# The last expert stage of a two-layer gated block: where the second product is scaled, and which engine does it

## The reference, cut to what matters

```
gate_scores = xf @ gate_W + gate_b
topk_scores, topk_idx = top_k(gate_scores, 2);  weights = softmax(topk_scores)
expert:  h = relu(layernorm(xf @ w1 + b1) * g1 + be1)
         layernorm(h @ w2 + b2) * g2 + be2
out = sum(weights * exp_out) + xf
x = x + tanh(g_ffn[1]) * out
```

## Time and profile before

| | us |
|---|---|
| median of 3 runs | 2147.1 |
| lowest and highest | 2144.46, 2152.93 |
| the profiled execution | 2151.43 |
| its span in the profile | 2149.6 |
| PE busy in the span | 2058.6 (96%) |
| DVE busy | 1737.7 (81%) |
| ACT busy | 1394.5 (65%) |
| POOL busy | 1269.6 (59%) |

### The profile page before, as it was taken

The page is one execution under the profiler, slowest core; times in us unless marked ns, Lnnn a source line. Parts: engine busy times, 40 slices in busy tenths (PEclk is TensorE's granted clock), DMA queues, the critical chain, the costliest instruction groups (busy, mean ns, idle before and its releaser), DMA issues.

```text
span 2149.6 us, 57692 instructions
## 1 busy us (share of the span) xinstructions
PE 2058.6 (96%) x19788; PEld 1795.7 (84%) x19788; DVE 1737.7 (81%) x4788; ACT 1394.5 (65%) x2978; POOL 1269.6 (59%) x2056
## 2 busy tenths in 40 slices
PE   6999999999699999999699999999899999999997
PEld 5888888888599999999588888888788888888885
DVE  5889888888588888888577787777588888888886
ACT  4766666666487877878366666666566666666663
POOL 5787888887300000000477878777378878878786
PEclk9999999999799999999899999999999999999998
DMA  7555221221466666666322222222100000000000
GB/s 230 187 180 166 67 65 61 69 64 53 158 239 226 247 223 246 221 244 213 133 69 71 71 75 71 75 71 66 45 23 30 29 28 29 30 30 30 30 26 18
DMA packets 151664, 226.11 MB, mean 105 GB/s; under 512 B 20454, under 2 KB 135786, under 8 KB 141036
## 3 DMA queue, kind: packets, MB, share of 16 engines
q1 hardware_dynamic: 145260, 205.99, 28.5%
q0 software_dynamic: 6144, 16.79, 2.5%
HBM read 153.77 MB, written 68.94 MB: 104 GB/s over the span
## 4 chain that ended last, share of the span: by engine, by line
PE 65%; DVE 15%; POOL 9%; issue 6%; DMA 3%; ACT 1%; POOLq 0%; SPq 0%; DVEq 0%; ACTq 0%
PE ps L1255 10%; PE ps L1271 10%; PE ps L1127 10%; PE ps L1112 6%; DVE u2g L1328 4%; PE ps L1066 4%; PE ps L1203 3%; PE ps L1215 3%; DVE h_st L1297 3%; PE ps L1159 3%; POOL k_rs L614 2%; PE ps L1083 2%; PE ps L1060 2%; PE ps L1096 2%; PE ps L1026 2%
## 5 line engine op out<-in xcount | busy, mean ns | idle before, releaser
L1397 DVE TENSOR_REDUCE nmax<-ps 128x16 f32<-128x2048 f32 x128 | 292.4, 2284 | 29.4 <-PE ps L1083 29.0
L874 ACT ACTIVATE prob_t<-ps 128x2048 f32<-128x2048 f32 x128 | 240.9, 1882 | 77.8 <-PE ps L1066 77.8
L696 POOL COPY slot_in<-slot_all 128x1 int32<-128x1 int32 x64 | 11.4, 179 | 472.9 <-DMA eo_d<-eo 472.9
L1026 PE MATMUL ps<-w2f,a_t 128*128 128x256 f32 x1024 | 233.3, 381 | 0.0
L1255 PE MATMUL ps<-xgt_hi,w_hl 128*128 128x256 f32 x1248 | 230.0, 282 | 1.0 <-DVE xgt_lo L1662 1.0
L1271 PE MATMUL ps<-w_hl,hid_hi 128*128 128x256 f32 x1248 | 226.9, 284 | 0.0
L1026 PEld LDWEIGHTS ps<-w2f,a_t 128*128 128x128 f32 x1024 | 190.9, 191 | 23.8
L670 POOL TENSOR_TENSOR km_r<-qk,cst 128x512 fp32r<-128x512 f32 x128 | 133.7, 1044 | 127.7 <-ACT qk L864 127.7
L946 ACT ACTIVATE hid<-ps,b_in 128x256 f32<-128x256 f32 x312 | 146.0, 469 | 82.6 <-PE ps L1255 67.2
L1255 PEld LDWEIGHTS ps<-xgt_hi,w_hl 128*128 128x128 f32 x1248 | 195.5, 189 | 1.4 <-issue 1.4
L1271 PEld LDWEIGHTS ps<-w_hl,hid_hi 128*128 128x128 f32 x1248 | 191.5, 188 | 0.0
(11 more groups left out here) (229 smaller groups left out, 6247.7 us busy)
## 6 DMA issues: line engine op xcount, KB each, us to landing
w_raw<-in_w_dram SPq DMA_DIRECT2D x78, 1024.0 KB, 6.8
c_t<-in_ctx_in_dram SPq DMA_DIRECT2D x128, 128.0 KB
x_d<-x SPq DMA_DIRECT2D x128, 128.0 KB
slots_d<-zeros SPq DMA_DIRECT2D x12, 1024.0 KB, 6.2
eo_d<-zeros SPq DMA_DIRECT2D x12, 1024.0 KB, 5.3
xg<-slots_d SPq DMA_DIRECT2D x39, 256.0 KB, 2.7
eo_d<-eo SPq DMA_DIRECT2D x39, 256.0 KB, 2.2
x_in<-in_x_dram SPq DMA_DIRECT2D x64, 128.0 KB
```

What stands on the lines that cost most here:

```text
L874: nc.scalar.activation(prob_t[:].rearrange("p a k -> p (a k)"), scores.rearrange("p a k -> p (a k)"), ACT.Exp, scale=SOFT).then_inc(y["exp ...
L1026: mm = pe.matmul(dst, a_t[:, b.parity, e, c, :], w2f[:, e, c, :], start=False, stop=True, skip_group_check=True)
L1397: nc.vector.tensor_reduce(nmax[:, b.parity, :, 0:4], scores.rearrange("p a (r k) -> p a r k", k=P), AX_X, ALU.max, negate=True).then_inc(y ...
```

## The change

```diff
-        u2g = psb("u2g", [P, E1, D])
+        u2g = psb("u2g", [P, 2, E1, D])
 ...
-                 ... u_done=4, be_done=1, ...
+                 ... u_done=2, u_scaled=4, be_done=1, ...
 ...  # GpSimd: k_rs, ahead of L612
-                        pool.wait_ge(f["u_done"].of(b - 1), f["u_done"].at(b - 1))
+                        pool.wait_ge(f["u_scaled"].of(b - 1), f["u_scaled"].at(b - 1))
 ...  # GpSimd: this block of s - 2 stood ahead of h_rs, and stands behind it now
+                b = s - 2
+                if b.within(B):
+                    pool.wait_ge(f["u_scaled"].of(b), f["u_scaled"].at(b))
+                    if (b - 1).begun:
+                        pool.wait_ge(f["summed"].of(b - 1), f["summed"].at(b - 1))
+                    nc.gpsimd.tensor_tensor(u2s[:], u2g[:, b.parity, 0:2, :], u2g[:, b.parity, 2:4, :], ALU.add).then_inc(f["halved"].sem, 1)
 ...  # ScalarE: between xft_hi (L778) and z1 (L786)
+                b = s - 2
+                if b.within(B):
+                    act.wait_ge(f["u_done"].of(b), f["u_done"].at(b))
+                    act.wait_ge(f["k_rstd"].of(b), f["k_rstd"].at(b))
+                    for e in range(E1):
+                        nc.scalar.activation(u2g[:, b.parity, e, :], u2g[:, b.parity, e, :], ACT.Copy, scale=k_rw[:, e:e + 1])\
+                            .then_inc(f["u_scaled"].sem, 1)
 ...  # TensorE: the wait ahead of the bias matmuls L1009
-                            pe.wait_ge(f["u_done"].of(b - 1), f["u_done"].at(b - 1, e + 2))
+                            pe.wait_ge(f["u_done"].of(b - 1), f["u_done"].at(b - 1, e // 2 + 1))
 ...  # VectorE: new
+            def out_of_psum(b, half):
+                if (b - 2).begun:
+                    dve.wait_ge(f["halved"].of(b - 2), f["halved"].at(b - 2))
+                two = slice(2 * half, 2 * half + 2)
+                nc.vector.tensor_tensor(u2g[:, b.parity, two, :].rearrange("p e n -> p (e n)"), ps[:, 6 + half, :],
+                                        g2_in[:, two, :].rearrange("p e n -> p (e n)"), ALU.mult).then_inc(f["u_done"].sem, 1)
 ...  # VectorE: the block of s - 2 with the four u2g (L1323 to L1330) is gone
 ...  # VectorE: b = s - 1
                     stats(6, k_st, f["k_stats"], f["down1_done"], b, 0)
+                    out_of_psum(b, 0)
 ...
                     stats(6, k_st, f["k_stats"], f["down1_done"], b, 1)
+                    out_of_psum(b, 1)
+                    if (b - 1).begun:
+                        dve.wait_ge(f["k_rstd"].of(b - 1), f["k_rstd"].at(b - 1, 1))
                     stats_in_all(k_st, k_mv, f["k_stats"], b)
```

More of the change, by code:

```diff
@@ L320, in flamingo_gated @@
         x4 = psb("x4", [P, 2, D])
-        late = 4096 + 4 * E1 * 6 // 4 + E1 * 2 + 2 * E1 + E1 + 4 * D + 2 * D + D + 2 * D + 2 * D + 2 * D
+        late = 5120 + 4 * E1 * 6 // 4 + E1 * 2 + 2 * E1 + E1 + 4 * D + 2 * D + D + 2 * D + 2 * D + 2 * D
         psb("gap1", [P, ATTENTION_WORDS - late])
@@ L420, in flamingo_gated @@
                  gexp_done=1, gate_mix=5, gwt_done=1, gw_turned=1, gw_t_done=1, up1_done=2, h_stats=8, h_rstd=2, z_act=4,
-                 z_turned=2, a_done=8, down1_done=2, k_stats=8, k_rstd=3, u_done=4, be_done=1, mixed_done=1, halved=1,
+                 z_turned=2, a_done=8, down1_done=2, k_stats=8, k_rstd=3, u_done=2, u_scaled=4, be_done=1, mixed_done=1, halved=1,
                  summed=2, mix=1))
@@ L636, in fstep @@
                     nc.gpsimd.tensor_tensor(gw8[:, b.parity, 0:E1], gwa[:], gwb[:], ALU.add).then_inc(f["gwt_done"].sem, 1)
[L637 to L642, removed]
                 b = s
@@ L1321, in fstep @@
                     nc.vector.tensor_scalar(gwb[:], iota_e[:, 0:E1], gidx[:, 1:2], gw[:, 1:2], ALU.is_equal, ALU.mult).then_inc(gm.sem, 1)
[L1322 to L1330, removed]
                 b = s
```

## The result

The changed kernel takes 2185.2 us (median of 4 runs, 2181.9 to 2187.9) against 2146.6 us for the kernel before, measured beside it (median of 4): a ratio of 1.0179, with a 95% interval of 1.0165 to 1.0192. It is slower by 38.6 us. The prediction was 2187 us, with a range of 2165 to 2207.

The account below looks back on a forecast made before the run. A circle through DVE and POOL was taken to set 9.07 us a step, PE nearly binding; the new circle's 9.75 gives 61 x 0.68 = +41.5, edges -1.3, sum +40: 2187 us, range 2165 to 2207.

Parts of the forecast that it names:

- PE alone: Step length if only PE's own work counted, without its waits for `z1`: about 8.85 us against 9.07.
- the 0.9 of the working: PE's forecast wait for `xf` in the changed kernel, about 0.9 us a step.
- The circle of the kernel before: Loop through DVE and POOL, said to set the old step of 9.07 us; 9.38 in the step shown.
- The circle: New loop from POOL's `k_rs` through `xf`, ACT's four scalings and `u2s` to the next `k_rs`: 9.70 us.
- The allowance of 0.05 for the turns: Added to the 9.70 us for turns of the loop and two more fulfilled waits on ACT, giving 9.75.
- `k_mv`'s circle: Loop from `k_mv` through `k_rs`, `xf`, L1026, statistics and the new DVE instruction: 9.34 us, covered by 9.70.
- The edges: Fill and drain outside the 61 steps: DVE +0.8 us, last L1026 earlier by 2.8; about -1.3 in all.
- Dear scalings: Rival: ACT's scaling starts lie 0.60 us apart, four take 2.40, time 2230 us; chance 0.12.
- halfway: Milder case of dear ACT scalings: starts 0.50 us apart, step 10.05 us, time 2207 us.
- The `k_mv` circle: Rival: cheaper scalings or a shorter POOL tail let the 9.34 us loop bind, 2165 us; chance 0.08.
- Not slower: Rival: early `u2s` and a cheap DVE pair leave PE the bound at 8.85 us, 2131 us; chance 0.10.
- The clock: Rival: PE's pauses lower its granted clock to 0.8 on average, 2267 us; chance 0.02.

Follow-up runs that it names:

- e5: Changed kernel with POOL's `u2s`, `u2t` and `rest` one step later and DVE's second PSUM instruction behind `k_mv`: 2137.5 us, ratio 0.9942 to 0.9966.
- e10: Changed kernel with POOL's sum one step later and both of DVE's new PSUM instructions behind `k_mv`: 2136.9 us, ratio 0.9937 to 0.9965.
- e2: Changed kernel with POOL's `u2s`, `u2t` and `rest` taken one step later, `u2s` ahead of `h_rs` again: 2162.7 us.
- e6: Changed kernel with POOL's `x4` moved ahead of `u2s`, into POOL's wait for ACT: 2160.8 us.
- e7: Changed kernel with POOL's order of before, `u2s` ahead of `h_rs`: 2340.2 us.
- e1: Changed kernel with DVE's second instruction out of PSUM behind `k_mv` instead of ahead of it: 2186.6 us.
- e9: Changed kernel with POOL's `x4` ahead of `u2s` and DVE's second PSUM instruction behind `k_mv`: 2140.2 us.
- e11: Changed kernel with four more ACT scalings, into a tile that nothing reads, ahead of the four: 2283.7 us.

## Why the prediction was right

*The frame.* DVE and POOL held the step at 9.07: before, POOL waits for `k_mv` and DVE for `k_rw` in every step. PE alone was put at 8.85, by taking off the waits of its weight loads; e5 and e10, with the chain of waits on PE, reached 8.96 and 8.92. So the room under 9.07 was 0.1 to 0.15 us rather than 0.22, and PE's wait for `xf` in the changed kernel is 0.73 us and not the 0.9 of the working. The circle of the kernel before was through `k_rw` and `u2g`, and the change did cut it, as the vanished wait shows.

*The circle, term by term.*

| piece | predicted | measured |
|---|---|---|
| `k_rs` to `xf` | 2.94 | 2.95 |
| `xf` to `xft_hi` | 1.16 | 1.13 |
| `xft_hi` to the first scaling | 0.28 | 0.28 |
| scalings, and on to `u2s` | 1.79 | 1.77 |
| `u2s` to `u2t` | 1.35 | 1.35 |
| `u2t` to `rest` | 0.80 | 0.81 |
| `rest` to `x4` | 0.69 | 0.68 |
| `x4` to `k_rs` | 0.69 | 0.71 |
| sum | 9.70 | 9.68 |

The price of the scaling rested on an instruction that ran once: 1.71 for four, 1.69 measured. The figure of the Trainium skill, "VectorE: DVE Perf Modes", section "The TRN2 errata — SBUF-src ops pay a fixed extra latency per instruction", would have made it an estimated 1.74; the measurement decides, and both are within 0.05. The DVE instruction lasts 0.67 us and takes 0.59 from start to start (0.692 and 0.61 predicted). The allowance of 0.05 for the turns came out as 0.065 (9.745 less 9.68).

*What was late next.* `k_mv`'s circle, 9.34 and 0.05: e2 and e6, in which POOL waits for `k_mv` again, stopped at 9.36 and 9.35. In e2's chain the first L1318 lies on it as well, through the input statistics; the working had only the second, and took the second product's last half as the start. Two ways of nearly one length.

*The edges.* The forecast was -1.3 us. Measured by the same points in both traces: from the first `frs` of the stage to the first L614, 24.16 against 24.45 us, -0.3; from the last of the 61 steps to the end of the span, 28.74 against 32.60, -3.9. The last L1033 starts 8.34 us after that point (before: 12.26) and lasts 3.72 us instead of 5.30; the granted clock is 1.00 over it, where before it was 0.66 in 2130 to 2135 us; 1.6 us of this is lost again while POOL finishes its tail. The forecast counted -2.8 for the start and nothing for the clock.

*The comparison of two executions.* The steps give 594.44 - 553.5 = +40.9, fill and drain -4.2, and the stage began 3.0 us earlier (1536.06 against 1539.05), in code that did not change; over the thirteen traces that start lies between 1533.6 and 1540.2. Together +33.7, the difference of the two spans (33.8) but for rounding. The medians differ by 38.6. So 2187 against 2185.2 owes something to errors that cancel; the step length, 9.75 against 9.745, does not.

*The rivals.* Dear scalings: no, 0.40 apart (halfway to them, at 10.05 us a step, the working's own terms give 2206 and not 2207). The `k_mv` circle: real, and the next to hold, 0.39 us a step behind. Not slower: it named the right two places, POOL's wait ahead of `u2s` and DVE's new pair on `k_mv`'s circle. e5 takes the wait away and one of the pair off that circle, e10 takes both off; they are faster, at 2137.5 and 2136.9 us, where the rival had 2131. The clock: 1.00 in the steps of the changed kernel; e7 has steps in which it falls.

## What to carry to other kernels

In a pipeline over several in-order engines, a move is priced by adding up the closed ways that it makes, from an instruction back to itself one step later, and not by the load of the engine that receives the work: ACT had been idle for over a third of the time in the steps (340.8 busy of 553.5 us), and the work given to it still cost 38 us, by standing between two things that POOL needed in one step. Try first to take the consumer of the new work one step later (e2), and then look for the second longest way, since an edit that frees it is worth nothing until the longest is gone (e1's edit alone gave 0, from e2 to e5 it gave 25 us and from e6 to e9 20).

## What was not expected of the hardware

In e7 PE's granted clock fell to its lower level (0.50, 1.2 GHz) in about three steps of five, about 1.6 us lost each time, where PE paused about 2.0 us in one piece in a step whose length without the drop is 11.3 us. In e11, with the same step and two pauses of 0.7 to 1.4 and 0.8 to 0.9 us, it stayed at 1.00. The Trainium skill, "TensorE: Matmul & The Clock Gate", section "Part 1: The HAM clock gate", says that the array is throttled by default and that activity releases it. e7 agrees as far as it goes: the clock falls behind a pause and comes back under work. What e11 adds is that the time paused per step, 1.9 us there against 2.0, doesn't decide by itself.
